# A fused attention and expert block: a new table of steps, two head groups per output bank, and a rebuilt opening

## What is computed

```python
scores = jnp.einsum('bqhd,bkhd->bhqk', qq, kk) * scale      # mla
scores = jnp.where(causal[None, None], scores, jnp.finfo(scores.dtype).min)
y = jnp.einsum('bhqk,bkhd->bqhd', jax.nn.softmax(scores, axis=-1), v).reshape(B, S, H)
...
scores, idx = jax.lax.top_k(jax.nn.sigmoid(xt @ W_router + routing_bias), TOPK)
combined = jnp.einsum('tei,eih,te->th', silu(g) * u, Wd_r, wts)
return (shared + combined).reshape(B, S, H)
```

## Time and profile before

| | us |
|---|---|
| three runs | 389.04, 391.2, 397.37 |
| median | 391.2 |
| the profiled execution: span from first to last instruction | 387.9 |
| PE busy in it | 337.9 (87%) |
| DVE, ACT, POOL busy | 286.0, 224.1, 122.7 |
| mean granted PE clock, share of full | 0.984 |

### The profile page before, as it was taken

The page is one execution under the profiler, slowest core; times in us unless marked ns, Lnnn a source line. Parts: engine busy times, 40 slices in busy tenths (PEclk is TensorE's granted clock), DMA queues, the critical chain, the costliest instruction groups (busy, mean ns, idle before and its releaser), DMA issues.

```text
span 387.9 us, 11664 instructions
## 1 busy us (share of the span) xinstructions
PE 337.9 (87%) x4504; PEld 205.0 (53%) x4504; DVE 286.0 (74%) x720; ACT 224.1 (58%) x545; POOL 122.7 (32%) x148
## 2 busy tenths in 40 slices
...
GB/s 193 82 197 100 26 155 43 89 56 65 27 22 160 24 69 54 84 167 3 64 41 30 58 65 48 43 6 161 3 2 0 3 0 27 3 28 0 30 0 27
DMA packets 29141, 21.84 MB, mean 56 GB/s; under 512 B 12312, under 2 KB 26008, under 8 KB 29048
## 3 DMA queue, kind: packets, MB, share of 16 engines
...
## 4 chain that ended last, share of the span: by engine, by line
PE 48%; DVE 28%; ACT 10%; issue 7%; SPq 3%; DMA 1%; ACTq 1%; POOL 1%; DVEq 0%; POOLq 0%
PE bank_B L1428 11%; DVE neg_max L1068 6%; PE bank_c L1332 6%; PE bank_A L1434 5%; PE bank_B L1236 5%; PE bank_A L1374 5%; ACT p_mla L886 3%; DVE s_loc L1085 2%; DVE row_max L1082 2%; ACT k_diag L830 2%; PE bank_M L1272 2%; SPq L624 1%; PE bank_M L1382 1%; DVE k_diag L1193 1%; PE bank_M L1397 1%
## 5 line engine op out<-in xcount | busy, mean ns | idle before, releaser
L886 ACT ACTIVATE p_mla<-bank_B 128x512 f32<-128x512 f32 (+1 forms) x176 | 94.3, 562 | 62.7 <-PE bank_B L1222 61.9
L1068 DVE TENSOR_REDUCE neg_max<-bank_A 128x1 f32<-128x512 f32 (+3 forms) x176 | 108.6, 637 | 19.5 <-PE bank_A L1222 15.8
L1236 PE MATMUL bank_B<-q_stack,k_stack 54*128 54x512 bf16 (+3 forms) x256 | 63.2, 303 | 10.9 <-DVE neg_max L1068 5.1
L1215 PE MATMUL bank_A<-k_stack,q_stack 52*128 52x512 bf16 (+3 forms) x256 | 63.7, 303 | 0.1
L1428 PE MATMUL bank_B<-xrT,k_diag 128*128 128x512 f32 x128 | 61.7, 600 | 1.2 <-DVE k_diag L1193 1.0
L759 POOL TENSOR_TENSOR x<-x,q_part 128x512 f32<-128x512 f32 x31 | 39.4, 1272 | 61.3 <-ACT q_part L920 43.0
L1332 PE MATMUL bank_c<-p_mla,v_mla 128*32 128x128 f32 (+12 forms) x512 | 47.5, 444 | 5.6 <-ACT p_mla L886 5.5
L1236 PEld LDWEIGHTS bank_B<-q_stack,k_stack 54*128 54x128 bf16 x256 | 19.2, 93 | 54.0 <-issue 23.1
L920 ACT ACTIVATE q_part<-bank_A,expert_w 128x128 f32<-128x128 f32 x108 | 30.8, 368 | 28.8 <-PE bank_A L1434 28.8
L1193 DVE SCALAR_TENSOR_TENSOR k_diag<-k_diag,bank_B 128x512 f32<-128x512 f32 x32 | 22.0, 687 | 31.5 <-ACT k_diag L904 30.3
L1222 PE MATMUL bank_A<-masks 64*128 64x64 bf16 (+2 forms) x352 | 43.1, 202 | 0.0
...
## 6 DMA issues: line engine op xcount, KB each, us to landing
...
```

What stands on the lines that cost most here:

```text
L886: drained_by(nc.scalar.activation(p_of(n)[:, m:m + len(heads), 0:w], src, ACT.Exp, scale=SCALE), step)
L1068: drained_by(nc.vector.tensor_reduce(neg_max[:, g, m:m + len(heads), i], src, AX.X, ALU.max, negate=True), step)
L1215: return nc.tensor.matmul(bank_of(step)[:, n * w:(n + 1) * w], q_stack[b % 2][rows, h % 8, i * P:(i + 1) * P], k_stack[b % 2][rows, h % 8, ...
L1236: nc.tensor.matmul(bank_of(step)[:, m * w:(m + 1) * w], k_stack[b % 2][rows, h % 8, j * P:(j + 1) * P], q_stack[b % 2][rows, h % 8, j * P: ...
```

## The change

- **The list** is written out as a string, `ORDER`, of 400 words and the counts of pairs between them (`*5` is five pairs). `SPREAD`, `merged` and the generators go. It holds the same steps, less eight `Y` steps. New is an assertion that `PICK.b.3` stands before `ROUTE.(b+1)`.
- **The opening**: `STATS.1` and `MV.0` stand before `MB.0`; `S` starts after `LV.0.1` and not after `LV.0.2`, `ST2` and `MV`; `ST2.0` comes after 11 pairs. Eleven pairs stand before `LS.0.0`, where before there were seven. Steps `XT.0.0`, `MA.0.1`, `LK.0`, `LQ.0` and `MV.0` use ring B. The tails of kT and qT go from DVE to ACT; the memsets of `s_loc` and `v_mla` go from DVE to POOL, and the second is now of the whole tile. ACT takes half of the `k_part` copies of batch 0, and rounds the middle part of the keys after them.
- **Two head groups per bank**: `v_mla` has 18 columns to a head, 9 zeros and then 8 values and the one. Group g = 0 (2) is taken from the values on, group 1 (3) from the zeros on, so that both add up in `bank_c` at rows 0 to 8 and 9 to 17 of each 32. The copy L895, the four transposes and the division happen for `Y.b.1` and `Y.b.3` only, each over twice as many heads. The heads of the weights are permuted in `WF` to match.

```diff
-        v_mla = sb("v_mla", [P, 2, NT, H, HD + 1])
+        v_mla = sb("v_mla", [P, 2, NT, H + 1, 2 * (HD + 1)])
-    if kind == "E":
+    if kind == "E" or step in EARLY_IN_B:
         return [("B", step)]
...
+            nc.gpsimd.memset(s_loc[:], 0.0).then_inc(ones_set, 1)
+            nc.gpsimd.memset(v_mla[:], 0.0).then_inc(v_mla_zeroed, 1)
+            pool.wait_ge(v_mla_zeroed, 1)
+            nc.gpsimd.memset(v_mla[:, :, :, 0:H, 2 * HD + 1:], 1.0).then_inc(ones_set, 1)
...
+                    if b == 0:          # ACT, step LK
+                        wait_drained(act, step)
+                        act.wait_ge(v_rows_set, 1)
+                        for par in range(2):
+                            for dst, src in k_halves(1, par):
+                                ins = nc.scalar.copy(dst, src)
+                        ins.then_inc(k_part_by_act, 1)
+                        act.wait_ge(rest_ready, 1)
+                        nc.scalar.copy(parts[:, 0, 1, :], rest[:]).then_inc(rounded[0], 1)
...
-                elif kind == "PV" and step[3] == NT - 1:
+                elif kind == "PV" and step[3] == NT - 1 and step[2] % 2:
...
-                    if j == 0 and n > 1:
-                        pe.wait_ge(c_drained, (n - 1) // NT)
+                    second = g % 2
+                    if j == 0 and not second and n > 1:
+                        pe.wait_ge(c_drained, (n - 1) // (2 * NT))
...
-                        first = (HD + 1) * (4 * g + m)
-                        width = min(PV_WIDTH, H * (HD + 1) - first)
+                        first = (HD + 1) * (2 * (4 * m + g) + 1 - second)
+                        width = min(PV_WIDTH, 2 * (HD + 1) * (H + 1) - first)
```

More of the change, by code:

```diff
@@ L149, in exp_units @@
     return [list(range(h, h + n)) for h in range(4 * g, 4 * g + 4, n)]
[L154 to L166, removed]
@@ L169, in merged @@
[L169 to L173, removed]
-def plan():
[L178 to L247, removed]
-    lists = [(experts(range(B)), *at["experts"][0]), (scores(), *at["scores"][0])]
-    for b in range(B):
-        lists += [(local(b), *at["local"][b]),
-                  (norm(b), *at["norm"][b]), ([("ST", b, n) for n in range(ST_PARTS)] if b else [], *at["stacks"][b]),
-                  ([("MV", b)], *at["values"][b]),
-                  ([("PICK", b, n) for n in range(PICK_PARTS)], *at["choice"][b])]
-    for b in range(1, B):
-        lists.append((project(b), *at["project"][b - 1]))
-        if b > 1:
-            lists.append(([("STATS", b)], *at["statistics"][b - 2]))
-    lists += [([("KD", 0, n) for n in range(KD_PARTS)], *at["keys"][0]), ([("ROOT",)], *at["root"][0])]
-    steps += merged(*lists)
@@ new lines @@
+PICK.0.0 PT.2.2 *2 LT.2.1 * PICK.0.1 PV.2.0.1 * SHIFT.2.2 LS.2.3 PV.2.0.2 LO.2.2 LR.2.3 PICK.0.2 *2 PT.2.3 LT.2.2
+LS.2.4 * MV.3 R2.1 * PV.2.0.3 KD.3.1 KD.3.2 KD.3.3 * PV.2.1.0 *2 ST.3.4 * ST.3.5 LO.2.3 *2 PICK.0.3 PV.2.1.1
+PV.2.1.2 * PV.2.1.3 *2 LR.2.4 SHIFT.2.3 R3.1 PT.2.4 * Y.2.1 VD.3.0 PV.2.2.0 * X2T.1 LT.2.3 LO.2.4 *2 LT.2.4 *2 LW.2
+LS.3.0 ST.3.6 LR.3.0 * ROUTE.1 PV.2.2.1 * PV.2.2.2 *2 PV.2.2.3 * PT.3.0 LS.3.1 * LO.3.0 LR.3.1 * PV.2.3.0 * PT.3.1 *
+ST.3.7 * SHIFT.3.0 * LT.3.0 LS.3.2 LO.3.1 VD.3.1 PV.2.3.1 * LR.3.2 PV.2.3.2 *2 PV.2.3.3 SHIFT.3.1 PT.3.2 * Y.2.3 *2
@@ new lines @@
+DOWN.1.0 GU.1.2 R3.3 DOWN.1.1 GU.1.3 DOWN.1.2 GU.1.4 DOWN.1.3 GU.1.5 DOWN.1.4 GU.1.6 PICK.2.1 PICK.2.2 DOWN.1.5
+X2T.3 GU.1.7 DOWN.1.6 PICK.2.3 ROUTE.3 GU.2.0 DOWN.1.7 GU.2.1 DOWN.2.0 PICK.3.0 PICK.3.1 GU.2.2 DOWN.2.1 GU.2.3
+PICK.3.2 DOWN.2.2 GU.2.4 DOWN.2.3 GU.2.5 DOWN.2.4 PICK.3.3 GU.2.6 DOWN.2.5 GU.2.7 DOWN.2.6 GU.3.0 DOWN.2.7 GU.3.1
+DOWN.3.0 GU.3.2 DOWN.3.1 GU.3.3 DOWN.3.2 GU.3.4 DOWN.3.3 GU.3.5 DOWN.3.4 GU.3.6 DOWN.3.5 GU.3.7 DOWN.3.6 DOWN.3.7
+"""
+def plan():
+    groups = [(b, g) for b in range(B) for g in GROUP_ORDER]
+    maxima = [("S", b, n) for b in range(B) for n in range(H // 4 * PER_GROUP)]
+    exps = [("E", b, g, j, u) for b, g in groups for j in range(NT) for u in range(len(exp_units(g, j)))]
+    pairs = [[step for of, at in ((maxima, n), (exps, n - LEAD * PER_GROUP)) if 0 <= at < len(of) for step in of[at:at + 1]]
+             for n in range(len(maxima) + LEAD * PER_GROUP)]
+    steps, sent = [], 0
+    for word in ORDER.split():
+        if word[0] == "*":
+            count = int(word[1:] or 1)
+            steps += [step for pair in pairs[sent:sent + count] for step in pair]
+            sent += count
+        else:
+            kind, *of = word.split(".")
+            steps.append((kind, *(int(n) for n in of)))
+    assert sent == len(pairs) and len(set(steps)) == len(steps)
@@ L261, in plan @@
     at = {step: n for n, step in enumerate(steps)}
     assert at["KD", 0, KD_PARTS - 1] < at["LS", 0, 0]
+    assert all(at["PICK", b, PICK_PARTS - 1] < at["ROUTE", b + 1] for b in range(B - 1))
     assert at["ROOT",] < min(at["LN", 1], at["STATS", 2], at["R2", 0])
@@ L798, in _ @@
                     drain(step, dst, bank[:], scale=cols[:, 3:4] if step[2] else None)
-                    if step == ("XT", 0, 0):
-                        act.wait_ge(rest_ready, 1)
-                        nc.scalar.copy(parts[:, 0, 1, :], rest[:]).then_inc(rounded[0], 1)
                 elif kind == "LQ":
```

108 lines of the change are left out of this document (68 added, 40 removed).

## The result

| | before | after |
|---|---|---|
| runs | 389.04, 391.2, 396.08, 397.37 | 372.07, 372.08, 373.04, 375.62 |
| median | 393.64 | 372.56 |
| span of the profiled execution | 387.9 | 370.3 |
| PE, DVE, ACT busy | 337.9, 286.0, 224.1 | 336.9, 280.7, 221.4 |
| mean granted PE clock | 0.984 | 0.965 |

What follows compares the result with a forecast made beforehand. PE was taken as a loose bound, often waiting behind DVE or ACT. Terms summed to -11.6 us from the profiled 387.9, a span of 376.3; runs lie 1.1 to 3.3 above, so 378.5, range 368 to 387.

Steps and rivals of the forecast that it cites:

- the deeper rival: Half of the 30.3 us of idle PE in the middle is filled, a run of 368.4 us; chance 0.22.
- Opening: Before the first S: S starts at 26.4 us, sooner by 2.4 us, between -4.1 and 0.
- Both signs: Opening wrong if weight copies begin later than 10 us, or the clock falls longer than before ahead of S.
- Eight Y steps fewer: PE loses 8 of 16 Y steps, 5.2 us, of which 0.8 counts: -4.1 us, between -5.2 and 0.
- YT and X1: One or two pairs between them in three batches remove three quarters of PE's waits there: -2.4 us.
- PV: More pairs before most PV cut PE's 5.5 us wait for exp tiles: -1.4 us, between -5.5 and +2.4.
- E and S behind DVE: PE's 8.8 us of waits for DVE's maxima and subtractions shrink as DVE has less work: -1.3 us.
- LT behind LO: Mean distance grows from 3.15 to 5.1 pairs, cutting the 1.3 us wait for y_loc: -1.0 us.
- SHIFT: Fewer pairs cover the way from SHIFT to E, so it gets tighter: +1.0 us, between 0 and +8.
- the rival of late maxima: Shifts find eight DMAs ahead in SP's queue and come late, a run of 400.9 us; chance 0.06.
- Experts: In the last stage R3.2, PICK.1.3 and ROUTE.2 move to other gaps: 0, between -1.8 and +3 us.
- DVE sets the pace: Waits removed at YT or PV return at the next maxima, a run of 386.4 us; chance 0.22.

Runs made afterwards that it cites:

- f5: e4 with 30 warming matmuls ahead of the first S instead of 10: 366.74 us, ratio 0.9231.
- e4: The changed kernel with the zeros of v_mla written by ACT instead of POOL: 371.48 us, ratio 0.9429.
- e1: The old list and opening with only two head groups per bank added, zeros by ACT: 393.63 us beside 394.47, ratio 0.9935.
- e2: The new list and opening with one head group per bank, Y.b.0 and Y.b.2 put back: 379.87 us, ratio 0.9653.
- g4: The changed kernel with one pair between Y.b.3, YT and X1 in batches 0 to 2: 380.06 us, ratio 0.9666.
- f7: The changed kernel with YT and X1 of batches 0 to 2 right behind Y.b.3: 388.53 us, ratio 0.9808.
- g3: g2 with YT two pairs behind Y.b.3 and X1 two behind YT: 389.69 us, ratio 0.9903.
- g2: e1 with each PV two pairs behind its last E: 398.05 us beside 393.62.
- f6: The changed kernel with each PV one pair behind its last E, as in the old list: 392.21 us, ratio 0.9888.
- g1: The changed kernel with each PV exactly two pairs behind its last E: 385.97 us, ratio 0.983.

## Why the prediction was right or wrong

**Sign and size.** Faster, as forecast, and inside the range, but in part by luck. The sum had -2.4 for the opening, -9.2 for the terms of the middle and 0 for the experts; the traces show +3.4, -18.8 and -2.2. The two large errors had opposite signs. f5, which mends the opening, takes 366.74, under the lower end of 368. The middle behaved as the deeper rival said: its idle time fell by 12.6 us (15.2 there), to 17.8 where my sum had "near 24 us". 372.56 also lies nearer to that rival's 368.4 than to my 378.5.

**Opening (-2.4).** Wrong, and this is the step with the wrong sign: +3.4 at the first E. "S at 26.4" failed by 2.6 us and "LS at 35.5" by 7.8. Three links of it failed. The memset was costed at nothing in the sum; it held DVE up for 1.16 us (e4). The late middle key part was seen ("ACT has more to do ahead of the middle key part"), and so was POOL's last one behind it, but not that DVE's last query part waits for POOL (1.12 us); "DVE's chain runs without a gap" was wrong there. And the clock had no price: I looked at when S starts, not at what PE does until then. The ten warming matmuls were done early, PE waited, the clock fell at 30.0, and the S units from the third on ran at half clock. e4 and f5 show the sizes: 1.9 us at the first E for the memset and the clock ahead of it, 4.7 for the clock behind the wait. With both the opening wins 3.2 us at the first E (58.4 against 61.6). Both signs that I had set for an error here came: the weight copies began at 10.62, later than 10 us, and the clock was at half for 17.1 us.

**Eight Y steps fewer (-4.1).** The busy times came near to what was computed: PE -4.7, ACT -4.6, DVE -2.5 where 1.3 was said. Its worth was mis-put as a share of PE's saving. Alone the ratio is 0.9935, about -2.6 us, with 1.1 of it in the middle (e1); in the new order it is 8.2 us of the middle. "Between -5.2 and 0" bounded it by PE's own matmuls. A Y step also held DVE idle at its reciprocal: 6.8 us before, 3.1 with the merge alone, 1.6 with the list alone, 0.7 with both. And it held PV for the copy of bank_c (2.5 us in e2). That last cost I had called zero, since the old trace did not show it: it is zero in the old order only.

**YT and X1 (-2.4).** The direction is right, its PE waits went (3.2 to 0.6). What the step is worth in the sum's sense was not measured, since no run puts the old neighbours back. What was measured is larger than 2.4 each time: 8.1 us of the middle for one pair in place of one or two (g4), 17.1 for nothing between (f7), 5.3 in the old order, mostly of clock (g3 against g2). The step that failed is "of 1.5 + 1.7 us of waits": it takes the bound engine's listed waits for the whole price. Not counted were DVE and ACT standing in order at X1 (DVE 4.0 us before, 0.7 after, 10.7 in f7), the maxima and exp tiles that come late after it, and the clock.

**PV (-1.4).** The same error. The wait for exp tiles went wholly (5.5 to none), though 6 of the 64 have no pair between; "six new ones at that price add 2.4" did not happen. Undone it costs 19.7 us (f6), of which 12.0 stay with two pairs (g1), where PE hardly waits for exp tiles. In the old order the same widening is no gain (g2). So PV's distance is not the mechanism by itself; its place among the steps is.

**E and S behind DVE (-1.3)**: 8.8 to 6.6 + 0.3 = 6.9, -1.9. Right in size, and that is luck: the reason given, less work for DVE, would shorten both waits, but the one for maxima rose (5.1 to 6.6) and the one for local subtractions nearly went (3.7 to 0.3). **LT behind LO (-1.0)**: 1.3 to 0.2, -1.1. Right. **SHIFT (+1.0)**: the wait for it went from 1.1 to 2.2 us, +1.1, under the threshold I had set (3 us). Right, and the rival of late maxima with its 20 us is refuted. **Experts (0)**: -2.2, a little outside "-1.8"; only 0.7 of it is PE's idle time (2.2 to 1.5), the rest its busy time, and one more pair stands ahead of GU.0.0 (196, not 195).

**DVE sets the pace.** Half true. It did not stop the gain, but what remains in the middle are waits for its maxima, and 175.2 of 207.7 us of DVE are busy there. I expect that a next step would have to take work from DVE; no run tries it.

**What stays open.** The middle wins at no single place, and not evenly. Counted by finished exp tiles, the kernel after is some 5 us ahead at tile 80 of 176 and 18 at the last, each from its first E. I did not find a rule that gives the time of a list from its distances. Regular places of PV (f6, g1, g2) lose each time, but no second irregular list was run, so whether the new table is a good one or only an irregular one isn't known. In f6 and g1 the clock is no large part of the loss (mean 0.98 in the middle, as after). In g2 (0.96) it is not separated from the order, and in f7 its part is worked out from its mean, not tested alone.
